# A macaron layer on eight cores: the layernorm before FFN 2 emitted in four groups within the attention's output projection

## What is computed

```python
def _layernorm(x, axis=-1, eps=1e-5):
    m = jnp.mean(x, axis=axis, keepdims=True)
    v = jnp.var(x, axis=axis, keepdims=True)
    return (x - m) / jnp.sqrt(v + eps)
# _act_quant: x to 8-bit steps by the row's largest magnitude; _weight_quant: w to -1, 0, 1 times a scale
def _bitlinear(x, w):
    return jnp.einsum('bsi,oi->bso', _act_quant(x), _weight_quant(w))
# ffn:  _bitlinear(silu(_bitlinear(x, w_gate)) * _bitlinear(x, w_up), w_down), 1024 -> 4096 -> 1024
# attn: 16 heads of 64, 4 key/value groups, causal softmax, then out @ Wp.T + bp
x = x + 0.5 * _L0_ffn_ref(_layernorm(x), w_gate, w_up, w_down)
x = x + _L0_attn_ref(_layernorm(x), Wq, Wk, Wv, Wp, bp)
x = x + 0.5 * _L0_ffn_ref(_layernorm(x), w_gate, w_up, w_down)
```

## Time and profile before

| | us |
|---|---|
| median of 2 runs | 4775.86 (4770.86 to 4780.86) |
| the profiled execution | 4766.55, of which its span on the slowest core, core 5, is 4764.7 |
| projection, first to last addition (core 5) | 3173.6 to 3275.7 |
| layernorm tiles | 3284.5 to 3440.6 |
| FFN 2, from its first product | 3448.7 to 4764.7 |

### The profile page before, as it was taken

One profiled execution on the slowest core, in us unless ns is written; L12 is line 12 of the kernel. 1 busy time (PEld: TensorE's weight loads), 2 busy tenths in 40 slices (PEclk: granted clock), 3 DMA queues, 4 the chain that ended last, 5 costly groups with the idle time before them and its releaser, 6 DMA issues.

```text
span 4764.7 us, 43102 instructions; the slowest of 8 cores (4731.9 to 4764.7 us)
## 1 busy us (share of the span) xinstructions
PE 2162.6 (45%) x10412; PEld 935.4 (20%) x10412; DVE 1717.7 (36%) x2419; ACT 935.0 (20%) x983; POOL 325.2 (7%) x476
## 2 busy tenths in 40 slices
PE   0010211001827374857625888853081635538387
PEld 0010111000313131322212333321030212213132
DVE  0123211710172626361113232214818374563801
ACT  3453644000101010100000666610010101001000
POOL 0120000022000000000000000000100000000000
PEclk9999999999968686978867555567596867769698
DMA  6535433223223232479842000043232222314588
GB/s 195 185 125 187 155 116 117 81 79 106 103 89 114 89 116 80 129 196 210 219 97 49 1 1 1 1 128 130 95 107 70 97 80 89 98 65 134 137 194 204
DMA packets 379689, 532.49 MB, mean 112 GB/s; under 512 B 248369, under 2 KB 271921, under 8 KB 375346
## 3 DMA queue, kind: packets, MB, share of 16 engines
q0 software_dynamic: 79616, 297.82, 19.5%
q1 hardware_dynamic: 261376, 132.18, 12.3%
q10 hardware_dynamic: 38450, 99.73, 6.0%
HBM read 365.01 MB, written 108.00 MB: 99 GB/s over the span
## 4 chain that ended last, share of the span: by engine, by line
PE 28%; DVE 26%; DMA 25%; ACT 9%; issue 7%; SPq 2%; ACTq 1%; POOL 1%; DVEq 1%; POOLq 0%
PE pu L689 8%; PE pg L676 7%; DMA wsl<-tuT 7%; ACT strips L966 4%; DMA q2t<-q2h 3%; PE app L954 3%; DVE fqh L733 3%; DVE t1h L736 3%; DVE ast L707 3%; PE pd L777 3%; PE apv L981 2%; SPq L54 2%; DMA wds<-tdT 2%; DMA wst_g<-wg 2%; DVE mbuf_q L463 2%
## 5 line engine op out<-in xcount | busy, mean ns | idle before, releaser
L676 PE MATMUL pg<-wsl,q1t 128*128 128x512 bf16 x2048 | 520.5, 400 | 1092.3 <-ACT sg L685 486.9
L689 PE MATMUL pu<-wsl,q1t 128*128 128x512 bf16 x2048 | 527.6, 404 | 184.3 <-DMA wsl<-tuT 184.3
L698 DVE TENSOR_TENSOR hb<-sg,pu 128x512 f32<-128x512 f32 x256 | 176.1, 688 | 951.2 <-PE pu L689 892.1
L685 ACT ACTIVATE sg<-pg,sgv 128x512 f32<-128x512 f32 x256 | 175.9, 687 | 1568.7 <-PE pg L676 892.2
L676 PEld LDWEIGHTS pg<-wsl,q1t 128*128 128x128 bf16 x2048 | 208.5, 102 | 1367.2 <-issue 1152.2
L777 PE MATMUL pd<-wds,q2t 128*128 128x512 bf16 x1024 | 286.3, 425 | 244.9 <-DMA wds<-tdT 181.4
L966 ACT ACTIVATE strips<-app,sc 128x1024 bf16<-128x1024 f32 x320 | 339.7, 1111 | 201.0 <-PE app L954 171.4
L954 PE MATMUL app<-qfm,kfm 64*128 64x512 bf16 x640 | 294.1, 578 | 77.9 <-ACT strips L966 55.8
L482 PE MATMUL stg<-identb,mbuf_q 128*128 128x128 bf16 x768 | 92.0, 308 | 467.8 <-DVE mbuf_q L463 467.8
L689 PEld LDWEIGHTS pu<-wsl,q1t 128*128 128x128 bf16 x2048 | 206.1, 102 | 469.4 <-issue 263.5
L463 DVE SCALAR_TENSOR_TENSOR mbuf_q<-pbuf_q,mbuf_q 128x2048 bf16<-128x2048 bf16 (+1 forms) x64 | 112.6, 1759 | 443.4 <-ACT mbuf_q L460 443.4
(11 more groups left out here) (124 smaller groups left out, 2169.8 us busy)
## 6 DMA issues: line engine op xcount, KB each, us to landing
wsl<-tgT POOLq DMA_DIRECT2D x64, 1024.0 KB, 7.7
wsl<-tuT POOLq DMA_DIRECT2D x64, 1024.0 KB, 5.7
wds<-tdT POOLq DMA_DIRECT2D x64, 1024.0 KB, 7.9
wst_d<-wd SPq DMA_DIRECT2D x64, 512.0 KB, 3.6
wst_g<-wg POOLq DMA_DIRECT2D x32, 1024.0 KB, 6.5
wst_u<-wu SPq DMA_DIRECT2D x32, 1024.0 KB, 5.6
q2h<-fqh ACTq DMA_DIRECT2D x32, 1024.0 KB, 3.8
xst<-x POOLq DMA_DIRECT2D x32, 512.0 KB, 6.1
```

The lines of the kernel that those rows point to most:

```text
L676: mk(P, "tensor", lambda e, f=f, sp=sp, j4=j4, s=sg_slot: e.matmul(pg[sp][:], q1t[:, f, j4 * 128:(j4 + 1) * 128], wsl[s][:, f, :], start=( ...
L685: mk(P, "scalar", lambda e, sp=sp, j=j: e.activation(sg[sp][:], pg[sp][:], AF.Silu, scale=sgv[:, j:j + 1]), reads=[b_pg[sp], b_sgv[j]], wr ...
L689: mk(P, "tensor", lambda e, f=f, sp=sp, j4=j4, s=su_slot: e.matmul(pu[sp][:], q1t[:, f, j4 * 128:(j4 + 1) * 128], wsl[s][:, f, :], start=( ...
L698: mk(P, "vector", lambda e, sp=sp, j4=j4, n=n: e.tensor_tensor(hb[:, j4, n * 512:(n + 1) * 512], sg[sp][:], pu[sp][:], ALU.mult), reads=[b ...
```

## The change

`emit_ln` gets an argument `dep`, on which its loads wait besides. `emit_attn` gets a callback, which it calls behind tiles 3, 7, 11 and 15 of the projection with the stores of these four tiles. The callback emits the layernorm of the four tiles from x2h and then their `finish_is1`. `emit_ffn(2, ...)` is handed the tokens of the q1h stores as `pre_q1`, and so emits no layernorm of its own. Both fences stay where they were, which puts all of the layernorm ahead of the second.

```diff
-        def emit_ln(src, tiles=None):
+        def emit_ln(src, tiles=None, dep=()):
...
                 mkdma(P, "gpsimd", xst[sx][:], src[j * 128:(j + 1) * 128, :],
-                      writes=[b_xst[sx]])
+                      writes=[b_xst[sx]], extra=list(dep))
...
-        def emit_attn(src, dst, pre_ln2=None):
+        def emit_attn(src, dst, pre_ln2=None, post_cb=None):
...
                     a_out_toks.append(mkdma(P, "scalar", dst[j * 128:(j + 1) * 128, :], xob[s][:], reads=[b_xob[s]]))
+                    if post_cb and j % 4 == 3:
+                        post_cb(j, a_out_toks[-4:])
...
                 P.fence()
-                emit_attn(x1h, x2h, pre_ln2=ln2_toks)
+                pre2 = []
+
+                def attn_cb(j, tks):
+                    pre2.extend(emit_ln(x2h, range(j - 3, j + 1), dep=tks))
+                    finish_is1(range(j - 3, j + 1))
+                emit_attn(x1h, x2h, pre_ln2=ln2_toks, post_cb=attn_cb)
                 P.fence()
-                final = emit_ffn(2, x2h, out_t)
+                final = emit_ffn(2, x2h, out_t, pre_q1=pre2)
```

## The result

| | us |
|---|---|
| before, beside the changed kernel | 4786.01 (10 runs) |
| changed kernel | 4829.37 (11 runs) |
| ratio | 1.0102, 95% interval 1.0067 to 1.0137 |
| ratio, both again later | 1.0110, 95% interval 1.0088 to 1.0131 (after_again, below) |

The account below looks back on a forecast made before the run. No engine is busy throughout: a row of stages, each with its own limit. Crossings 34 plus fence 12 make 46 us: 4812 on the profiled 4766.55, 4822 on the median 4775.86; predicted 4820, range 4798 to 4845.

Parts of the forecast that it names:

- The order in the queues: In the projection, ScalarE's load of tile 4 queues behind the group's four square roots, so nothing of consequence overlaps.
- rival (a): In the projection, the overlap works: gaps vanish beneath layernorm, 40 us less, 4736; chance 6%.
- The crossings, 34 us: Switches to layernorm and back after tiles 3, 7 and 11 add 11.2 us each, 34 for three.
- The round trip: At each crossing, end of additions to first layernorm operation, by store and reload through HBM: 8.79 us.
- From layernorm to additions: Behind a group's fourth layernorm tile, additions start at about 7.0 us, after square roots, load issue and landing.
- the 0.5: Tile after a crossing: TensorE computes at its low clock level, step 7.14 us instead of 6.63, 0.5 more.
- The fence, 12.2 us: Second fence: transposed q1t loads wait for the last finish; TensorE starts 20.3 us after layernorm instead of 8.1.
- FFN 2, nothing: FFN 2 runs the same instructions from a cold start as before; costed at nothing.
- Rival (b): At the second fence, q1t's loads are quick and cost nothing: +34 to +36 us, 4811; chance 10%.
- Rival (c): TensorE stays at the low clock level through all the projection: 12 us more, 4832; chance 8%.
- Rival (d): FFN 2's first group runs at the low clock, slower by over 2%: 4920 or 4928; chance 2%.
- What would show it: Timeline signs: TensorE idle some 51 us per crossing, load about 2.7 us behind layernorm, tile 1 to layernorm's end about 293.

Follow-up runs that it names:

- after_again: The changed kernel run again, with a second trace; ratio to the kernel before 1.0110.
- 3a: The changed kernel with all 16 finishes (square roots) moved behind the second fence; ratio to the kernel before 1.0075.
- 3b: The changed kernel with two buffers of its own for the projection's x1h loads, same place in ScalarE's queue; ratio to the kernel before 1.0113.
- e7: The changed kernel with the same prefetch of the projection's x1h loads as e5; ratio to the kernel before 1.0067.
- e5: The kernel before with the projection's x1h loads requested ahead into four buffers from SyncE's queue, and two axob; ratio to the kernel before 0.9943.
- Experiment 5: The kernel before, unchanged, traced twice more for FFN 2's length, compared with the variants' traces; 1313.6 and 1318.1 us.
- e1: The changed kernel with layernorm as one block behind the projection, still ahead of the second fence; ratio to the kernel before 1.0069.
- e2_again: Second run of the changed kernel with its fourth layernorm group moved behind the second fence; ratio to the kernel before 1.0093.
- e8: e6 without its prefetch: x1h loads in two own buffers in ScalarE's queue, one axob; ratio to the kernel before 0.9902.
- e6: e5's prefetch with layernorm tile by tile, two behind; last two tiles and all finishes behind the second fence; 4706.94 us, ratio to the kernel before 0.9868.

## Why the prediction was right, and where its terms were off

The forecast was 4820, +46 us; measured were +43 in the medians, 1.0% in the ratio (49 us), and 52 in the three stages above. Sign and mechanism held. The sum came out near by some luck: the crossings were put 9 us too high, the fence 4 too low and FFN 2, at nothing, 11 too low. The terms, in its own order:

- *The order in the queues.* Right: ScalarE's load stands behind the square roots, experiments 3a and 3b show that it is this order and not the buffer, and rival (a) falls with them. Nothing overlapped: VectorE was simply idle in other places.
- *The crossings, 34 us.* Over-sized: 24.6 measured. The round trip took 7.7 us on average, not the 8.79 that was read on one core at the end (8.4 over the cores, and ahead of it GpSimd had the fence to pass). From layernorm to additions it took 6.0, not 7.0: ScalarE requests the load 2.4 us after layernorm, with the last square root under way, and the additions begin 3.6 us after the request, less than the 4.1 that a load takes in the projection's steady state. The gap between two tiles' additions that is saved is 5.15 us, as said (in the kernel before, tiles 4, 8 and 12 come 6.63 us after the tile ahead of them, less 1.48). The step behind a crossing is 7.0 us, more than the mean, but the same three steps took 7.2 in the kernel before, which has no crossings (why they are long there is not shown): the 0.5 were nothing. That makes 7.7 + 6.0 - 5.15 = 8.5 a crossing, 25.6 for three, less 0.7 for the last group's shorter round trip, 24.9. The fit that was cited from the Trainium skill (DMA: Bandwidth & Descriptors, Anatomy of one DMA — SWDGE (gpsimd) path) is stated there for DMAs issued by GpSimd, so it bears on the reload and not on ScalarE's store.
- *The cause of that last term* was mistaken. TensorE does run at its low level behind each crossing (3.57 us for eight products). But in the rows above the tile after was released by a DMA at 3251.37, not by TensorE: the step waits for its load, as most steps do in both kernels. Only where loads are early does TensorE's restart show: e7's four tiles take 16.9 us and e5's 15.7.
- *The fence, 12.2 us.* Under-sized: 16.4. The row that was used for it (17.0 us from SyncE's first transposed load to TensorE) was of the right kind, but the shortest of its kind: over all cores, traces and groups of the kernel before this wait is 17.0 to 23.5 us, 19.1 on average, and in the changed kernel it was 20.1. SyncE began 4.3 us after layernorm, not 3.3. On 12 of the 16 cores traced VectorE went on straight from its last finish, which ended at 3.4 us, and SyncE's first load was issued 0.8 us later, a step that the prediction left out. On the other four, core 2 of the rows above among them, the last store of q1h was late (landed after 4.0 to 5.1 us, where 3.0 were said) and held the fence.
- *FFN 2, nothing.* 11 us longer in the traces. Experiment 5 shows that the other variants have it too, and that a lower granted clock goes with it; the cause stays open.
- *Rival (b)*, a free fence, is refuted by e1 and by the start times of 8.5 and 24.6 us in e2_again and after_again. *Rival (c)*: the clock came back within a tile or two at each crossing, and the steps that stand neither first nor behind a crossing are 6.6 us in both kernels. *Rival (d)*: the first group of FFN 2 takes 162.4 us in the changed kernel and 161.9 before, from first product to the start of the next group; the clock there is no loss.
- *What would show it*: idle TensorE 49.91 us (51 said), a load 2.47 us behind the last layernorm operation (2.7 said), from the additions of tile 1 to the end of layernorm 290 us on core 2 (293 said). These were seen. But one of the signs of being wrong was seen too: FFN 2 was to stay within 15 us of 1316, and on the slowest core it took 1334.8 us, 19 more (1332.9 in after_again). The sum hides it, as the crossings were over-sized by nearly as much.

## What to carry to other kernels

Idle time of an engine is filled only by work that stands in its own queue between the two operations that wait for each other. Emitting the next stage in blocks puts the block's own latency into the middle and lets every queue that the block uses (here ScalarE's, with its square roots, and VectorE's, with the finishes) hold back the stage that it interrupts. Software-pipelined tile by tile, two tiles behind, the same work gained 1.0% without a prefetch (e8) and 1.3% with one (e6), instead of losing 1.0%. And work that is moved ahead of a barrier takes its cover with it: look at what used to run beside it, here eight transposed loads, and leave a last piece behind the barrier for them to run under.

## What the runs showed of the hardware

The latency of one and the same 512 KB transfer depended on what ran beside it. The store of x2h took 2.9 us in the median with one load requested right behind it, 5.7 with the next tiles' loads requested ahead (e5), 7.5 with loads, stores and reloads together (e6). A prefetch thus lengthens the latencies that are still on a chain: in e7 the round trips at the three crossings took 10.1 us on average and the last, with no load left to request, 7.1 (7.7 in the changed kernel). The eight transposing loads show the same: they took 10.05 us to issue during layernorm and 18.11 beside three weight loads in the changed kernel.
